# Macaron attention: the first q projection ahead of the scores on PE, and its rotation ahead of the maxima on DVE

## The chip, the cores and the metric

The kernel runs on one core of a Trainium2 chip. A core has five engines with a queue each: PE (TensorE, matmuls and transposes into PSUM), DVE (VectorE), ACT (ScalarE), POOL (GpSimd) and SP (SyncE, which here only issues DMAs). Each engine takes its instructions in program order; between engines there are semaphores. The metric is the device time of one execution in microseconds (us).

## What is computed

The input is 2 sequences of 1024 tokens with 128 features, in float32. Six sublayers follow each other, each behind a layer norm: a half-weighted "macaron" block, a linear attention, the same macaron block again, a mixture of experts, a full attention, and the experts again. The change touches the macaron block, which runs twice. It has 6 layers, each an attention over windows of 32 tokens in 16 heads and a gated feed-forward network. Its attention, cut to what matters:

```python
def attn_layer(x, Wqkv, qs, ksc, Wo):
    q, k, v = jnp.split(x @ Wqkv, 3, -1)             # 128 -> 3 x 1024
    q = l2norm(q) * qs                               # per head of 64
    k = l2norm(k) * ksc
    q = q * cos * scale + rotate_half(q) * sin * scale
    k = k * cos * inv + rotate_half(k) * sin * inv
    out = local_attention(q, k, v)                   # softmax over 64 keys
    return out @ Wo
...
for i in range(DEPTH):                               # 6
    x = attn_layer(shift_tokens(x), ...) + x
    x = ffn_layer(shift_tokens(x), ...) + x
```

## The kernel before

Tokens are cut into 16 tiles of 128. The macaron block is one pipeline over 6 x 16 = 96 tiles (`NT`), written out as 106 steps. Each engine runs the same loop `step(s)` in its own function, `macaron_pe`, `macaron_act`, `macaron_dve` and `macaron_pool`, and the order of the work is the order in which these functions issue it. In step s several tiles are in hand at once: tile u = s+2 is projected, squared and rotated, k = s+1 is scaled and transposed, t = s has its scores and softmax, o = s-1 is multiplied with the values and projected out, v = s-3 and z = s-4 have their layer norm for the feed-forward network.

A tile's q and k are each projected in two halves of 512 columns (the first and the second 32 of each head's 64 features), so `project_qk(u, q)` is called with q = 0 to 3, where 0 and 1 are the halves of q. Each of the four goes to a PSUM bank, ACT squares it out of there into `sq` (L554, for the norms), and DVE's `rotate(u, q)` (L666) multiplies it out of there with two rows of the rotary tables into `turn1` and `turn2`. POOL adds the two (L811) and, one step later, `scale(k, w)` (L795) multiplies the sum with the reciprocal norms `rn` into `qkr`, which PE transposes (L392). `turn1` and `turn2` exist once for q and once for k. That is why `rotate` has, for q = 0 and 2, a wait on the semaphore `qk_rotated` of the tile before:

```python
dve.wait_ge(sem("squared"), part(n, "squared", q))
if on(n - 1) and a == 0:
    dve.wait_ge(sem("qk_rotated"), part(n - 1, "qk_rotated", w))
```

POOL's order in a step is `scale(k, 0)`, `scale(k, 1)`, the normalisation of the probabilities (L823), the two adds (L811), a small `off` (L831) and the tables of the tile after (`ropes`, L805). The `off` waits for the end of DVE's Newton iteration in this step (L687), so that the next step's `scale(k, 0)` stands behind this iteration, the `off` and the `ropes`.

The scores of tile t (L417, 128 small matmuls) lie in two PSUM banks. DVE takes their row maxima (`nmax`, L724) and subtracts them into `scratch` (L729); ACT takes the exponential (L591); DVE sums it (`den`, L746) and inverts it (L749).

The feed-forward network works on groups of four tiles. Its gate matmuls (L462) with their gelus on ACT (L576, with a load of ACT's function table before and after, L579 behind it), its up matmuls (L469) with DVE's products (L702), and its output matmuls (L479) with DVE's addition (L708) stand at the end of three successive steps, and the fourth step has none. Below, a step is named by what the step before it ended with: behind a gate, behind an up, behind an out, and behind none.

`refill(b, ...)` is PE's bookkeeping of a PSUM bank: it waits until the last content was read. Bank 2 serves projections 0 and 3 and the first parts of gate and up.

Of the kernel before, what the change touches and what calls it, by code (L numbers as in the profile page):

```python
# [99 lines left out]
def build(nc, x_in, W, const, maskc, out):  # L100
    with ExitStack() as ctx:
# [233 lines left out]
        def on(n):  # L335
            return 0 <= n < NT
# [18 lines left out]
        def macaron_pe(pe, c):  # L355
# [9 lines left out]
            def project_qk(n, q):  # L365
                b = QK_BANK[q]
                refill(b, ("turned", part(n, "turned", q)))
                w, a = q // 2, q % 2
                w0 = INNER * w + RH * a
                pe.matmul(bank[b][:, :], xT[:, n // TPB % 2, bass.ts(n % TPB, P)],  # L370
                          wqkv[n // TILES % 2][:, INNER * w:INNER * w + INNER].rearrange(
                              "p (h a d) -> p h a d", a=2, d=RH)[:, :, a, :],
                          start=True, stop=True).then_inc(sem("projected"), 1)
# [110 lines left out]
            def step(s):  # L484
                x, u, k, t, o, v, z = s + 3, s + 2, s + 1, s, s - 1, s - 2, s - 4
                if s >= NT:
                    feed_forward(s)
                if on(t):
                    scores(t)
                if on(u):  # L490
                    if u % TILES == 0:
                        layer = DEPTH * c + u // TILES
                        pe.wait_ge(sem("attn_weights%d" % (layer % 2)), 16 * AW * (layer // 2 + 1))
                    pe.wait_ge(sem("xT_kept"), part(u, "xT_kept"))
                    for q in range(3):
                        project_qk(u, q)
                if on(o):
                    pe.wait_ge(sem("pT_kept"), part(o, "pT_kept", 1))
                    pe.wait_ge(sem("v_kept"), part(o, "v_kept", 1))
                    pe.wait_ge(sem("values_paired"), at.paired(o))  # L500
                    for i in range(2):
                        refill(OUT_BANK[i], ("aT_kept", part(o, "aT_kept", i)))
                    attend(o, 0)
                if on(k):
                    turn_qk(k, 0)
                if on(o):
                    attend(o, 1)
                if on(u):
                    project_qk(u, 3)
                if on(k):  # L510
                    project_v(k, 0)
                    turn_qk(k, 1)
                    turn_qk(k, 2)
                    project_v(k, 1)
                    turn_qk(k, 3)
                if on(t):
                    turn_p(t, 0)
                    turn_p(t, 1)
                if on(o):
                    project_out(o)  # L520
                if on(x) or on(z):
                    b = MIX_BANK
                    filled = []
                    if on(x):
                        filled.append(("xT_kept", part(x, "xT_kept")))
                    if on(z):
                        filled.append(("xnT_kept", part(z, "xnT_kept")))
                    refill(b, *filled)
                    if on(x):
                        if x >= TILES:  # L530
                            pe.wait_ge(sem("unit_added"), at.group((x - TILES) // 4, "unit_added"))
                        mm = pe.transpose(bank[b][:, 0:P], Y[:, x % TILES, :], ident[:, :])
                    if on(z):
                        pe.wait_ge(sem("unit_normed"), part(z, "unit_normed"))
                        mm = pe.transpose(bank[b][:, ZN_AT:ZN_AT + P], zn[:, :], ident[:, :])
                    mm.then_inc(sem("mixed"), 1)
                if s < NT:
                    feed_forward(s)
# [110 lines left out]
        def macaron_dve(dve, c):  # L649
# [67 lines left out]
            def step(s):  # L717
                u, t, o, v, z = s + 2, s, s - 1, s - 3, s - 4
                if s >= NT:
                    feed_forward(s)  # L720
                if on(t):
                    dve.wait_ge(sem("scores"), part(t, "scores"))
                    both = psum[:, S_BANK[0]:S_BANK[0] + 2, :].rearrange("p a b -> p (a b)")
                    dve.tensor_reduce(nmax[:, :], both.rearrange("p (h k) -> p h k", k=NWIN), AX.X, ALU.max,  # L724
                                      negate=True).then_inc(sem("maxima"), 1)
                    dve.wait_ge(sem("maxima"), part(t, "maxima"))
                    if on(t - 1):
                        dve.wait_ge(sem("p_turned"), part(t - 1, "p_turned", 1))
                    dve.tensor_tensor(prob[:, :].rearrange("p (h e k) -> p e h k", e=2, k=NWIN),  # L729
                                      both.rearrange("p (e h k) -> p e h k", e=2, k=NWIN),  # L730
                                      nmax[:, :].rearrange("p (e h) -> p e h", e=2).unsqueeze(3).broadcast_to(
                                          [P, 2, PAIRS, NWIN]), ALU.add).then_inc(sem("centred"), 1)
                if on(v):
                    dve.wait_ge(sem("shifted%d" % (v % 2)), at.shifted(v))
                    dve.bn_stats(st6[:, 0, :], Y[:, v % TILES, 0:HALF])
                    dve.bn_stats(st6[:, 1, :], zs[:, v % 2, :]).then_inc(sem("unit_stats"), 1)
                if on(u):
                    rotate(u, 0)
                if on(v):
                    dve.wait_ge(sem("unit_stats"), part(v, "unit_stats"))  # L740
                    if on(z):
                        dve.wait_ge(sem("unit_offset"), part(z, "unit_offset"))
                    dve.bn_aggr(mv[:, :], st6[:, :, :]).then_inc(sem("unit_moments"), 1)
                if on(t):
                    dve.wait_ge(sem("exp_done"), part(t, "exp_done"))
                    dve.tensor_reduce(den[:, :], prob[:, :].rearrange("p (h k) -> p h k", k=NWIN), AX.X,  # L746
                                      ALU.add).then_inc(sem("totals"), 1)
                    dve.wait_ge(sem("totals"), part(t, "totals"))
                    dve.reciprocal(rden[:, :], den[:, :]).then_inc(sem("inverted"), 1)  # L749
                if on(u):  # L750
                    rotate(u, 1)
                    rotate(u, 2)
                    rotate(u, 3)
                if s > FIRST_STEP:
                    dve.wait_ge(sem("rnorm"), at.step(s - 1))
                if on(v):
                    dve.wait_ge(sem("unit_moments"), part(v, "unit_moments"))
                    dve.tensor_scalar(ss[:, 32:33], mv[:, 1:2], LN_EPS, 64.0 / 9.0, ALU.add, ALU.mult).then_inc(
                        sem("unit_var"), 1)
                if on(u):  # L760
                    lengths(u, 0)
                    lengths(u, 1)
                    dve.wait_ge(sem("summed"), part(u, "summed", 1))
                    dve.tensor_scalar(ss[:, 0:32], ss[:, 0:32], 1e-24, None, ALU.max).then_inc(sem("norms_squared"), 1)
                    dve.wait_ge(sem("norms_squared"), part(u, "norms_squared"))
                if on(v):
                    dve.wait_ge(sem("unit_var"), part(v, "unit_var"))
                if on(z):
                    dve.wait_ge(sem("unit_normed"), part(z, "unit_normed"))
                if on(u - 1):  # L770
                    dve.wait_ge(sem("qk_rotated"), part(u - 1, "qk_rotated", 1))
                dve.tensor_scalar(rn[:, :].bitcast(I32), ss[:, :].bitcast(I32), -0.5, MAGIC, ALU.mult,
                                  ALU.add).then_inc(sem("guessed"), 1)
                dve.wait_ge(sem("guessed"), at.step(s))
                rsqrt(s)
                if on(o):
                    dve.wait_ge(sem("attn_out"), part(o, "attn_out"))
                    dve.tensor_tensor(Y[:, o % TILES, :], bank[WO_BANK][:, 0:D], Y[:, o % TILES, :],
                                      ALU.add).then_inc(sem("attn_added"), 1)
                if s < NT:  # L780
                    feed_forward(s)
# [871 lines left out]
```

## Time and profile before

| | |
|---|---|
| median of 3 runs | 4118.94 us (4118.94 to 4139.54) |
| the profiled execution | 4144.42 us |
| its span, first to last instruction | 4142.6 us |
| PE busy | 3870.5 us (93%) |
| DVE busy | 3321.1 us (80%) |
| ACT busy | 2742.4 us (66%) |
| POOL busy | 2224.1 us (54%) |
| mean granted TensorE clock | 0.953 of full speed |

The busy times are sums over the whole span, so they don't say which engine another waits for. The chain of work that ended last is followed back from the last instruction; the profile puts 63% of it on PE and 27% on DVE. In rows of the timeline, "x6" means six instructions merged into one row, the first number is the start in us from the span's start, the second the length in us, and the bracket at the end says how long the engine sat idle before the row and what ended that.

### The profile page before, as it was taken

How to read it: one execution, taken by the hardware profiler on the slowest of the kernel's cores; microseconds unless marked ns; L12 is line 12 of the kernel's file. 1: busy time of each engine (PE TensorE's matmuls, PEld its weight loads, DVE VectorE, ACT ScalarE, POOL GpSimd, SP SyncE). 2: the span in 40 equal slices, each digit the busy share in tenths (PEclk: the TensorE clock that was granted, in tenths of full speed). 3: DMA queues.
4: the chain of work that ended last, by engine and by line, in shares of the span. 5: the costliest groups of instructions: out<-in, count | busy, mean ns of one | idle time of the engine just before them, and what ended most of it. 6: DMA issues, size and time to landing. Idle time of an engine off the chain costs nothing.

```text
span 4142.6 us, 151779 instructions
## 1 busy us (share of the span) xinstructions
PE 3870.5 (93%) x65521; PEld 2410.0 (58%) x65521; DVE 3321.1 (80%) x6608; ACT 2742.4 (66%) x4984; POOL 2224.1 (54%) x1394
## 2 busy tenths in 40 slices
PE   6999999999999999589999999999999977999985
PEld 3666666666666666356666666666666654333333
DVE  7988888888888888588888888888888865577745
ACT  4777777777767676167777777777777742466662
POOL 4766666666666665077666666666666630000000
PEclk8999999999999999799999999999999987599996
DMA  3112121121121211012211211212111110000000
GB/s 103 41 35 57 40 57 40 40 57 40 35 57 40 57 38 43 23 29 45 51 41 40 57 40 40 57 40 57 35 43 38 35 26 0 1 1 1 1 1 11
DMA packets 138056, 154.51 MB, mean 37 GB/s; under 512 B 74392, under 2 KB 97320, under 8 KB 135728
## 3 DMA queue, kind: packets, MB, share of 16 engines
q1 hardware_dynamic: 137392, 144.81, 15.2%
q8 instruction: 520, 8.52, 0.9%
q14 instruction: 144, 1.18, 0.1%
HBM read 36.71 MB, written 1.05 MB: 9 GB/s over the span
## 4 chain that ended last, share of the span: by engine, by line
PE 63%; DVE 27%; issue 6%; ACT 2%; POOL 0%; DVEq 0%; SPq 0%; POOLq 0%; DMA 0%; ACTq 0%
DVE turn L666 10%; PE psum L381 10%; PE psum L449 8%; PE psum L392 8%; PE psum L417 7%; DVE nmax L724 5%; DVE den L746 5%; PE psum L441 4%; PE psum L1297 3%; PE psum L462 3%; PE psum L1285 3%; PE psum L469 3%; PE psum L479 3%; PE psum L370 2%; PE psum L1287 2%
## 5 line engine op out<-in xcount | busy, mean ns | idle before, releaser
L666 DVE TENSOR_TENSOR turn<-psum,ropes 128x512 f32<-128x512 f32 x1536 | 938.5, 672 | 31.4 <-ACT sq L554 27.1
L811 POOL TENSOR_TENSOR turn<-turn 128x1024 f32<-128x1024 f32 x384 | 904.6, 2377 | 32.6 <-DVE turn L666 32.5
L554 ACT ACTIVATE sq<-psum 128x512 f32<-128x512 f32 x768 | 451.5, 594 | 500.3 <-PE psum L370 498.9
L370 PE MATMUL psum<-wqkv,xT 128*128 128x512 f32 x1536 | 773.2, 626 | 8.5 <-DVE turn L666 6.8
L795 POOL TENSOR_TENSOR qkr<-turn,rn 128x1024 f32<-128x1024 f32 x384 | 727.9, 1918 | 17.3 <-DVE rn L687 17.2
L823 POOL TENSOR_TENSOR scratch<-scratch,rden 128x1024 f32<-128x1024 f32 x192 | 365.7, 1904 | 657.4 <-DVE rden L749 657.4
L392 PEld LDWEIGHTS psum<-ident,qkr 128*128 128x128 f32 x3072 | 329.4, 142 | 334.5 <-ACT kT L563 156.3
L392 PE MATMUL psum<-ident,qkr 128*128 128x128 f32 x3072 | 467.0, 285 | 6.7 <-POOL qkr L795 6.0
L692 DVE TENSOR_REDUCE ss<-sq 128x16 f32<-128x1024 f32 x384 | 447.9, 1207 | 0.0
L428 PEld LDWEIGHTS psum<-scratch,Vs 64*64 64x64 f32 x12288 | 330.4, 135 | 197.6 <-issue 197.2
L381 PE MATMUL psum<-wqkv,xT 128*64 128x512 f32 x1536 | 420.2, 626 | 23.2 <-DVE turn L666 6.1
L1423 DVE TENSOR_REDUCE gel<-psum 128x1 f32<-128x1024 f32 x256 | 303.9, 1220 | 150.8 <-PE psum L1266 149.4
L724 DVE TENSOR_REDUCE nmax<-psum 128x16 f32<-128x1024 f32 x192 | 235.0, 1224 | 232.2 <-PE psum L417 231.9
L428 PE MATMUL psum<-scratch,Vs 64*64 64x32 f32 x12288 | 395.6, 223 | 21.5 <-issue 21.5
L370 PEld LDWEIGHTS psum<-wqkv,xT 128*128 128x128 f32 x1536 | 263.7, 191 | 224.2 <-issue 182.2
L428 PE MATMUL psum<-scratch,V 64*64 64x32 f32 x12288 | 388.2, 220 | 0.5 <-issue 0.5
L449 PE MATMUL psum<-wo,aT 128*128 128x128 f32 x3072 | 377.5, 276 | 2.6 <-ACT aT L607 2.6
L449 PEld LDWEIGHTS psum<-wo,aT 128*128 128x128 f32 x3072 | 361.2, 193 | 2.8 <-ACT aT L607 2.8
L567 ACT ACTIVATE V<-psum 128x512 f32<-128x512 f32 x384 | 229.7, 598 | 190.8 <-PE psum L381 190.8
L428 PEld LDWEIGHTS psum<-scratch,V 64*64 64x64 f32 x12288 | 332.8, 137 | 0.6 <-issue 0.6
L417 PEld LDWEIGHTS psum<-kT,qT 64*32 64x32 f32 x24576 | 255.4, 105 | 91.1 <-issue 72.1
L417 PE MATMUL psum<-kT,qT 64*32 64x64 f32 (+1 forms) x24576 | 287.0, 225 | 4.5 <-ACT psum L625 3.5
(193 smaller groups left out, 6536.4 us busy)
## 6 DMA issues: line engine op xcount, KB each, us to landing
Vs<-V SPq DMA_DIRECT2D x384, 128.0 KB
Vs<-V SPq DMA_DIRECT2D x768, 64.0 KB
wqkv<-in_L_ffn_Wqkv_dram SPq DMA_DIRECT2D x12, 1536.0 KB
wo<-in_L_ffn_Wo_dram SPq DMA_DIRECT2D x48, 128.0 KB
zs<-Y SPq DMA_DIRECT2D x192, 31.8 KB
w<-in_L_ffn_W_dram SPq DMA_DIRECT2D x12, 341.0 KB
zs<-Y SPq DMA_DIRECT2D x168, 0.2 KB
w<-in_L_ffn_W_dram SPq DMA_DIRECT2D x12, 128.0 KB
```

The costliest lines, as they stand in the source:

```text
L370: pe.matmul(bank[b][:, :], xT[:, n // TPB % 2, bass.ts(n % TPB, P)], wqkv[n // TILES % 2][:, INNER * w:INNER * w + INNER].rearrange("p (h ...
L381: mm = pe.matmul(bank[b][DH * e:DH * e + DH, :], xT[:, n // TPB % 2, t0:t0 + 64], wv[:, :, e, :], start=True, stop=True, skip_group_check= ...
L392: mm = pe.transpose(bank[b][:, P * j:P * j + P], qkr[:, w, P * p:P * p + P], ident[:, :])
L417: mm = pe.matmul(out, q, keys, start=False, stop=True, skip_group_check=True)
L428: mm = pe.matmul(bank[OUT_BANK[e]][o0:o0 + DH, P * i + WIN * w:P * i + WIN * w + WIN], v[r0:r0 + NWIN, w // 2, p, :], pT[r0:r0 + NWIN, p, ...
L449: mm = pe.matmul(bank[WO_BANK][:, 0:D], aT[:, p, :], wo[n // TILES % 2][:, p, :], start=(p == 0), stop=(p == PAIRS - 1))
L554: act.activation(sq[:, q // 2, q % 2, :, :], bank[QK_BANK[q]][:, :].rearrange("p (h d) -> p h d", d=RH), ACT.Square).then_inc(sem("squared ...
L666: e = dve.tensor_tensor(dst, src, tab.unsqueeze(1).broadcast_to([P, HEADS, RH]), ALU.mult)
L692: dve.tensor_reduce(ss[:, 16 * w:16 * w + 16], sq[:, w, :, :, :].rearrange("p a h d -> p h a d"), AX.XY, ALU.add).then_inc(sem("summed"), 1)
L724: dve.tensor_reduce(nmax[:, :], both.rearrange("p (h k) -> p h k", k=NWIN), AX.X, ALU.max, negate=True).then_inc(sem("maxima"), 1)
L795: pool.tensor_tensor(qkr[:, w, :].rearrange("p (h a d) -> p a h d", a=2, d=RH), turn1[:, w, :, :, :], r.unsqueeze(1).unsqueeze(3).broadcas ...
L811: pool.tensor_tensor(t1, t1, turn2[:, w, :, :, :].rearrange("p a h d -> p (a h d)"), ALU.add).then_inc(sem("added"), 1)
```

## The change

PE issues `project_qk(u, 0)` ahead of `scores(t)`, and projections 1 and 2 stay behind them. DVE issues `rotate(u, 0)` as the first thing of the step (behind a feed-forward part only in the last steps), ahead of the maxima. ACT's and POOL's programs and all waits inside the moved functions stay as they are.

```diff
@@ macaron_pe, step(s)
-                if on(t):
-                    scores(t)
                 if on(u):
                     if u % TILES == 0:
                         layer = DEPTH * c + u // TILES
                         pe.wait_ge(sem("attn_weights%d" % (layer % 2)), 16 * AW * (layer // 2 + 1))
                     pe.wait_ge(sem("xT_kept"), part(u, "xT_kept"))
-                    for q in range(3):
-                        project_qk(u, q)
+                    project_qk(u, 0)
+                if on(t):
+                    scores(t)
+                if on(u):
+                    project_qk(u, 1)
+                    project_qk(u, 2)
@@ macaron_dve, step(s)
+                if on(u):
+                    rotate(u, 0)
                 if on(t):
                     dve.wait_ge(sem("scores"), part(t, "scores"))
...
-                if on(u):
-                    rotate(u, 0)
                 if on(v):
                     dve.wait_ge(sem("unit_stats"), part(v, "unit_stats"))
```

On PE, at the border of two steps behind an out (the transposes L532 and L535 and the output matmuls L479 close the old step; `kT,qT` are the scores, `wqkv1,xT` the projections), this stood there before:

```order
L535 MATMUL psum<-ident,zn 128x128 [waits unit_normed]
L479 MATMUL psum<-w20,gT 128x128 [waits gated,qk_kept]
L479 MATMUL psum<-w20,gT 128x128 x3
L417 MATMUL psum<-kT,qT 32x64 [waits qk_kept,masked]
L417 MATMUL psum<-kT,qT 32x64 x63
L370 MATMUL psum<-wqkv1,xT 128x512 [waits turned,xT_kept]
L370 MATMUL psum<-wqkv1,xT 128x512 [waits v_kept] x2
```

And this stands there now:

```order
L537 MATMUL psum<-ident,zn 128x128 [waits unit_normed]
L479 MATMUL psum<-w20,gT 128x128 [waits gated,qk_kept]
L479 MATMUL psum<-w20,gT 128x128 x3
L370 MATMUL psum<-wqkv1,xT 128x512 [waits turned,xT_kept]
L417 MATMUL psum<-kT,qT 32x64 [waits qk_kept,masked]
L417 MATMUL psum<-kT,qT 32x64 x63
L370 MATMUL psum<-wqkv1,xT 128x512 [waits v_kept] x2
```

One projection of 512 columns has moved ahead of the scores.

On DVE, from the end of the Newton iteration (L687; L689 now) and the up products (L702; L704 now) into a step behind an up, this stood there before:

```order
L687 SCALAR_TENSOR_TENSOR rn<-rt,rn 128x33 [waits newton]
L778 TENSOR_TENSOR Y<-psum,Y 128x128 [waits attn_out]
L702 SCALAR_TENSOR_TENSOR gT<-psum,b1,gel 128x512 [waits gelu,unit_up] x2
L702 SCALAR_TENSOR_TENSOR gT<-psum,b1,gel 85x512 [waits gelu,unit_up]
L724 TENSOR_REDUCE nmax<-psum 128x16 [waits scores]
L729 TENSOR_TENSOR scratch<-psum,nmax 128x2x8x64 [waits p_turned,maxima]
L735 BN_STATS st6<-Y 128x6 [waits shifted1]
L736 BN_STATS st6<-zs 128x6
L666 TENSOR_TENSOR turn1<-psum,ropes0 128x512 [waits ropes_scaled,qk_rotated,squared]
L666 TENSOR_TENSOR turn2<-psum,ropes0 128x512
L743 BN_AGGR mv<-st6 128x2 [waits unit_offset,unit_stats]
L746 TENSOR_REDUCE den<-scratch 128x16 [waits exp_done]
```

And this stands there now:

```order
L689 SCALAR_TENSOR_TENSOR rn<-rt,rn 128x33 [waits newton]
L780 TENSOR_TENSOR Y<-psum,Y 128x128 [waits attn_out]
L704 SCALAR_TENSOR_TENSOR gT<-psum,b1,gel 128x512 [waits gelu,unit_up] x2
L704 SCALAR_TENSOR_TENSOR gT<-psum,b1,gel 85x512 [waits gelu,unit_up]
L668 TENSOR_TENSOR turn1<-psum,ropes0 128x512 [waits ropes_scaled,qk_rotated,squared]
L668 TENSOR_TENSOR turn2<-psum,ropes0 128x512
L728 TENSOR_REDUCE nmax<-psum 128x16 [waits scores]
L733 TENSOR_TENSOR scratch<-psum,nmax 128x2x8x64 [waits p_turned,maxima]
L739 BN_STATS st6<-Y 128x6 [waits shifted1]
L740 BN_STATS st6<-zs 128x6
L745 BN_AGGR mv<-st6 128x2 [waits unit_offset,unit_stats]
L748 TENSOR_REDUCE den<-scratch 128x16 [waits exp_done]
```

The two rotations, with their three waits, have moved ahead of the maxima, and nothing is left between the centring (L729; L733 now) and the sum of the exponentials but the small statistics.

## Rows read from the trace of the kernel before

**Rows 1.** Who waited for whom (us in total, times, longest us), and the page's part 5
```profile
L724 DVE TENSOR_REDUCE nmax<-psum 128x16 f32<-128x1024 f32 x192 | 235.0, 1224 | 232.2 <-PE psum L417 231.9
PEld psum L381 <- DVE turn L666: 176.6, 190, 3.6
```
**Rows 2.** The chain that ended last, in order of time, one step
```profile
1039.93 1.23 DVE turn L666 x2
1041.21 1.08 PE psum L381 x4
...
1051.97 1.19 DVE turn L666 x2
```
**Rows 3.** Timeline of DVE, the step behind none, and the other three kinds' maxima
```profile
1017.17 1.22 DVE L724 TENSOR_REDUCE nmax<-psum 128x16 f32<-128x1024 f32 x1 [0.67 <-PE psum L417]
...
1034.60 1.23 DVE L724 TENSOR_REDUCE nmax<-psum 128x16 f32<-128x1024 f32 x1 [0.83 <-PE psum L417]
...
1049.23 1.22 DVE L724 TENSOR_REDUCE nmax<-psum 128x16 f32<-128x1024 f32 x1 [0.49 <-PE psum L417]
1050.49 1.22 DVE L729 TENSOR_TENSOR scratch<-psum,nmax 128x1024 f32<-128x1024 f32 x1
...
1053.20 1.16 DVE L746 TENSOR_REDUCE den<-scratch 128x16 f32<-128x1024 f32 x1
...
1054.57 3.61 DVE L666 TENSOR_TENSOR turn<-psum,ropes 128x512 f32<-128x512 f32 x6
...
1066.44 1.23 DVE L724 TENSOR_REDUCE nmax<-psum 128x16 f32<-128x1024 f32 x1 [3.09 <-PE psum L417]
```
**Rows 4.** Timeline of PE: scores behind up, out and none; the step behind none
```profile
1015.65 1.48 PE L417 MATMUL psum<-kT,qT 64*32 64x64 f32 x128
...
1032.97 1.59 PE L417 MATMUL psum<-kT,qT 64*32 64x64 f32 x128
...
1047.72 1.48 PE L417 MATMUL psum<-kT,qT 64*32 64x64 f32 x128
1049.13 2.84 PE L370 MATMUL psum<-wqkv,xT 128*128 128x512 f32 x6
...
1054.62 1.12 PE L370 MATMUL psum<-wqkv,xT 128*128 128x512 f32 x2
1055.84 1.08 PE L381 MATMUL psum<-wqkv,xT 128*64 128x512 f32 x4
...
1059.38 1.04 PE L441 MATMUL psum<-ident,scratch 128*128 128x128 f32 x8
```
**Rows 5.** Timeline of ACT: the step behind none, and the squares behind a gate
```profile
1050.29 0.60 ACT L554 ACTIVATE sq<-psum 128x512 f32<-128x512 f32 x1 [1.42 <-PE psum L370]
...
1051.75 1.06 ACT L591 ACTIVATE scratch<-scratch 128x1024 f32<-128x1024 f32 x1
...
1068.19 1.09 ACT L554 ACTIVATE sq<-psum 128x512 f32<-128x512 f32 x2
```
**Rows 6.** Timeline of POOL: the border into the step behind none
```profile
1048.64 0.27 POOL L831 TENSOR_SCALAR off<-mv,rn 128x1 f32<-128x1 f32 x1 [1.96 <-DVE rn L687]
...
1049.54 3.79 POOL L795 TENSOR_TENSOR qkr<-turn,rn 128x1024 f32<-128x1024 f32 x2
```
**Rows 7.** Timeline where the second macaron block begins: DVE waits for the exponential
```profile
1788.62 1.06 ACT L591 ACTIVATE scratch<-scratch 128x1024 f32<-128x1024 f32 x1
1789.71 1.22 DVE L746 TENSOR_REDUCE den<-scratch 128x16 f32<-128x1024 f32 x1 [1.23 <-ACT scratch L591]
```
**Rows 8.** Timeline of PE behind two waits at the beginnings of the blocks
```profile
66.28 1.97 PE L381 MATMUL psum<-wqkv,xT 128*64 128x512 f32 x4 [1.45 <-DVE turn L666]
...
1792.41 1.27 PE L381 MATMUL psum<-wqkv,xT 128*64 128x512 f32 x4 [2.75 <-DVE turn L666]
...
1797.52 1.04 PE L441 MATMUL psum<-ident,scratch 128*128 128x128 f32 x8
```
**Rows 9.** PE's busy time, granted clock and DMA in stretches of 1 us
```profile
1794.00:1795.00 1.00, 1.00 (x7) 0.50 0.00 0
```

## The prediction

> **What bounds the kernel now.** The page's busy shares don't settle it, so I read the waits first. The largest visible wait of DVE in the macaron block is the one for the scores, 231.9 us before 192 maxima, 1.2 us a step; and PE in turn waits 176.6 us, about 0.9 us a step, for DVE's rotation before it projects the values [rows 1]. Two engines that wait for each other in every step are one loop. The chain of waits shows it: DVE's rotation 1, then PE's value projection at once, from there PE's tail of the step up to the next scores, the maxima, and over rotation 0 to the next rotation 1 [rows 2]. The step before is therefore (rotation 1 to scores, on PE) + (scores) + (maxima to rotation 1, on DVE), and anything put on this loop costs its full length. The DVE wait for scores that the change fills with a rotation is real, but it is a link of the loop, not free time beside it.
>
> **The change, part by part.** No instruction is added or removed. I take one group of four steps from the middle of the first block, in which each kind of step occurs once.
>
> *What is saved.* Today rotation 0 lies between the centring and the sum of the exponentials, from the maxima to rotation 1 it is 1054.57 - 1049.23 = 5.34 us [rows 3]. Without rotation 0 the sum must wait for ACT: maxima to centring 1.26 [rows 3], centring to the start of the exponential 1051.75 - 1050.49 = 1.26 [rows 3, 5], exponential to sum 1.09, as where DVE really waited for it [rows 7], sum to rotation 1 1.37 [rows 3]. That is 4.98 us. So of the 1.19 us of rotation 0 [rows 2] only 0.36 us come off this stretch; the rest was cover for the exponential, and the cover is gone.
>
> *What is added ahead of the maxima.* Rotation 0 now needs three things before it may start, and the maxima stand behind it in DVE's queue even when the scores are ready.
> (a) Its projection and square. From a projection's start to the start of its square it is 1050.29 - 1049.13 = 1.16 us, the square takes 0.60 [rows 4, 5], I add 0.03 to hand it on (the exponential needed that [rows 7]) and 1.19 for the rotation: 2.98 us from PE's start to the maxima. Now it is the scores alone, about 1.5 us. On PE itself the scores end two passes (0.86 us) later, at about 2.4, which this hides.
> (b) The buffer. `turn1` and `turn2` of q are read by POOL's `scale(k, 0)`. Behind none POOL comes to it at 1049.54, with `off` and `ropes` ahead of it, and two take 3.79, so the first ends at 1051.44 [rows 6]. Today nobody sees that, because rotation 0 comes 2.7 us behind the start of the maxima. Now it stands between DVE and maxima that could have started at 1049.23.
> (c) Behind a gate, ACT. The gelus and two table loads lie ahead of the first square in ACT's queue, and it starts only at 1068.19 [rows 5], 1.75 us behind the start of the maxima today.
>
> New starts of the maxima, against those of today [rows 3 to 6]:
> - behind none: 1051.44 + 0.06 + 1.19 = 1052.69 for 1049.23, +3.46, net of the 0.36 +3.10
> - behind a gate: 1068.19 + 0.60 + 0.03 + 1.19 = 1070.01 for 1066.44, +3.57, net +3.21
> - behind an up: 1015.65 + 2.98 = 1018.63 for 1017.17, +1.46, net +1.10
> - behind an out: 1032.97 + 2.98 = 1035.95 for 1034.60, +1.35, net +0.99
>
> Everything from rotation 1 on (PE's tail, DVE's reductions and Newton iteration, POOL's adds, ACT's copies and gelus) hangs on rotation 1 as before, so a delay is not made up later in the step; the periods just grow. In the up step the products L702 free bank 2 before PE gets to it, which I cost at nothing; the cover is PE's own matmuls, without it it is some tenths.
>
> In a block rotation 0 and maxima share steps s = 0 to 93: 30 behind none, 22 behind a gate, 21 behind an up, 21 behind an out. For two blocks: 60 x 3.10 + 44 x 3.21 + 42 x 1.10 + 42 x 0.99 = 186 + 141 + 46 + 42 = **415 us**. SP's queue is not moved, and its pairing DMAs get more time, which can give back a few us.
>
> *The clock.* PE's wait before the value projections grows with the same amounts. Behind none, projection 3 starts at 1054.62, its two passes take 0.86, and the next matmul starts at 1055.84 [rows 4]: 0.4 us of gap today, 3.5 then, 3.6 behind a gate, about 1.4 in the other two. What such waits do is shown where the blocks begin: behind a wait of 2.75 us the clock stood at 0.50, the lower of its two levels (1.2 GHz), while PE worked, and the way from the value projection to the transposes of the probabilities took 1797.52 - 1792.41 = 5.11 us, against 1059.38 - 1055.84 = 3.54 in the middle: 1.57 us lost [rows 4, 8, 9]. Behind a wait of 1.45 us the same projection took 1.97 instead of 1.08 [rows 8], so even that can be enough. The bounds for the block's middle: 0 (today's gaps of 0.4 us leave the clock at full) and all of them. A fall costs where PE's tail or ACT behind it decides the next maxima, in tails with gate, up or out: 44 + 44 + 42 steps. In the tail without one, PE has 1052.69 - (1047.72 + 2.98) = 1.99 us in hand behind POOL, and 1.57 fits in. Those with gate or up (88) follow a long gap, those with out a short one. I take nine in ten of the 88 and a quarter of the 42, at 1.5 us because a fall sometimes begins before the wait ends: 90 x 1.5 = **135 us**. The most is 130 x 1.57 = 204 us.
>
> The Trainium skill, "TensorE: Matmul & The Clock Gate", section "HAM oscillation", tells of a kernel in which PE had to wait in every turn of a loop and came back at half rate in every one. By that rule all 88 long gaps fall and the term is 88 x 1.57 = 138 us; a reading of the middle of the blocks alone, where gaps are 0.4 us, would leave it at 0. The rows at the blocks' beginnings side with the page.
>
> **Sum.** 415 + 135 = 550 us. On the profiled execution's own 4144.4 us that is 4694; the median lies 25.5 us lower, so I forecast **4669 us**.
>
> **The rivals.**
> 1. *The loop as above, the clock stays at 2.4 GHz* (PE's attention matmuls in front of the gap may count for enough): 4119 + 415 = 4534 us. For it: both rows of a fall come from the first steps of a block, where these attention matmuls are missing. Against it: one of these waits was only 1.45 us [rows 8]. Chance 0.20.
> 2. *More than forecast*: every gap brings a fall, or one outlasts the tail and slows the next scores too. From 4119 + 415 + 204 = 4738 us up, to some 4850 if half of the falls cost double. Chance 0.12.
> 3. *POOL and ACT don't stand in the way*, because their work moves ahead when steps get longer; then only (a) is left in all kinds: 188 x 1.1 = 207, 4326 us. Against it: POOL's `scale` is tied to this loop's Newton iteration through `off`, which waited 1.96 us for it [rows 6]. Chance 0.07.
> 4. *The other side, faster*: the rotation fits into DVE's wait for the scores and the maxima don't get later, so 0.36 us a step are won, 188 x 0.36 = 68 us: 4051 us. It decides if both the square and `qk_rotated` are there 1.2 us before the scores end. Behind a gate DVE did sit idle for 3.09 us [rows 3], but there the square would have to end at 1065.2 and ends at 1068.8, and behind none the buffer would have to be free at 1048.0 and is at 1051.4. Chance 0.03.
> 5. *No effect*, the two amounts cancelling or the loop not being the bound: 4119 us. The chain of waits speaks against it. Chance 0.02.
>
> My own case has 0.56, with 4600 to 4738 as its range. A measurement of this kernel tells about 0.5% from no change. Cases 1, 2, 3 and mine are all slower: slower 0.95, same 0.02, faster 0.03. The range for 8 in 10 takes in mine and most of 1 and of 2: from 4520 to 4770 us.
>
> **What the changed profile would show.** The wait of the maxima for the scores is gone from the list (231.9 us), since the maxima now follow the rotation directly. In its place rotation 0 waits for `qkr` (POOL L795) behind none, some 2.7 us each time, and for the square elsewhere, most behind a gate. The sum of the exponentials waits some 0.7 us for ACT in every step. PE's wait for the rotation before the value projections grows from 0.9 us to about 3 on average. In the middle of a block four steps take 3.10 + 3.21 + 1.10 + 0.99 = 8.4 us more than now, or 11.5 with the clock's part (two long gaps at nine in ten and a short one at a quarter, 1.5 us each), and the granted clock there is below 1.00. The forecast is wrong if rotation 0 doesn't wait for POOL, or if four steps grow by less than 8 us; if they grow by just 8.4, rival 1 holds.

## The result, and the profile after

The changed kernel takes 4574.11 us (median of 4, 4553.43 to 4584.89), the kernel before, run beside it, 4129.24 us (4118.94 to 4140.34). The ratio is 1.108 with a 95% interval of [1.104, 1.112], slower by 445 us. The forecast was 4669 us with a range of 4520 to 4770: the direction and the range held, the size was 95 us too high, and rival 1 (the same loop without the clock's part, 4534 us) came closer.

The waits of the changed kernel, in us in total, times, longest:

```profile
PEld psum L381 <- DVE turn L668: 468.8, 194, 5.2
DVE turn L668 <- ACT sq L556: 347.5, 144, 6.3
PE psum L381 <- DVE turn L668: 311.5, 180, 4.3
DVE turn L668 <- POOL qkr L797: 150.2, 56, 2.8
DVE den L748 <- ACT scratch L593: 122.1, 192, 1.1
```

The wait of the maxima for the scores, 231.9 us in [rows 1], has shrunk to 2.4 us. In its place DVE waits 498 us ahead of rotations: 144 times for the square, 56 times for POOL's scaling of the tile before, and about nine in ten of these waits stand ahead of rotation 0. A third one, 0.62 us in most steps, is the bubble in front of the sum of the exponentials. PE's wait for DVE before the value projections has grown from 176.6 to 468.8 us, which is 2.4 us each and not the 3 us forecast.

One group of steps in the timeline of DVE: behind none, behind a gate, behind an up, behind an out.

```profile
1098.40 1.22 DVE L728 TENSOR_REDUCE nmax<-psum 128x16 f32<-128x1024 f32 x1
...
1115.02 1.29 DVE L668 TENSOR_TENSOR turn<-psum,ropes 128x512 f32<-128x512 f32 x2 [2.81 <-POOL qkr L797]
1116.22 1.22 DVE L728 TENSOR_REDUCE nmax<-psum 128x16 f32<-128x1024 f32 x1
...
1119.82 1.22 DVE L748 TENSOR_REDUCE den<-scratch 128x16 f32<-128x1024 f32 x1 [0.62 <-ACT scratch L593]
...
1121.24 3.62 DVE L668 TENSOR_TENSOR turn<-psum,ropes 128x512 f32<-128x512 f32 x6
...
1137.07 1.29 DVE L668 TENSOR_TENSOR turn<-psum,ropes 128x512 f32<-128x512 f32 x2 [6.29 <-ACT sq L556]
1138.28 1.22 DVE L728 TENSOR_REDUCE nmax<-psum 128x16 f32<-128x1024 f32 x1
...
1155.26 1.29 DVE L668 TENSOR_TENSOR turn<-psum,ropes 128x512 f32<-128x512 f32 x2 [0.74 <-ACT sq L556]
1156.46 1.22 DVE L728 TENSOR_REDUCE nmax<-psum 128x16 f32<-128x1024 f32 x1
...
1173.54 1.29 DVE L668 TENSOR_TENSOR turn<-psum,ropes 128x512 f32<-128x512 f32 x2 [0.80 <-ACT sq L556]
1174.75 1.22 DVE L728 TENSOR_REDUCE nmax<-psum 128x16 f32<-128x1024 f32 x1
```

Every maxima row now starts the moment its rotation is through; what the rotation waited for stands in the bracket. From the starts of all 192 maxima I took the period of each step, that is from the start before to its own, and sorted them by kind (the first maxima of a block have no period, so it is 58 of the 60 behind none):

| step behind | before, median | worked out | after, median | steps |
|---|---|---|---|---|
| none | 14.63 | 17.73 | 17.83 | 60 |
| a gate | 17.22 | 20.43 | 20.48 | 44 |
| an up | 17.22 | 18.32 | 18.18 | 42 |
| an out | 17.32 | 18.31 | 18.29 | 42 |

The medians account for 60 x 3.20 + 44 x 3.26 + 42 x 0.96 + 42 x 0.97 = 416 us. The rest are steps above their kind's median. Behind a gate 16 of 44 lie at 22.0 to 23.4 us, behind an up 9 at 19.5 to 21.1. PE's timeline shows the one behind a gate of the group above, with PE's granted clock in 1 us:

```profile
1111.92 1.12 PE L370 MATMUL psum<-wqkv,xT 128*128 128x512 f32 x2 [0.65 <-ACT xT L635]
...
1119.05 1.13 PE L370 MATMUL psum<-wqkv,xT 128*128 128x512 f32 x2
1122.52 1.75 PE L381 MATMUL psum<-wqkv,xT 128*64 128x512 f32 x4 [2.34 <-DVE turn L668]
1124.20 1.97 PE L392 MATMUL psum<-ident,qkr 128*128 128x128 f32 x8
...
1127.64 1.04 PE L441 MATMUL psum<-ident,scratch 128*128 128x128 f32 x8
```
```profile
1124.00:1125.00 1.00, 1.00 (x6) 0.50 0.87 194
```

Behind the wait the clock is at the lower level, and from the value projection to the transposes of the probabilities it takes 1127.64 - 1122.52 = 5.12 us, as at the block's beginning [rows 8], instead of 3.54 [rows 4]. Only it happened much less often than I had taken it to. In the record of the granted clock there are 33 falls (154 us) between the first and the last maxima of the two blocks, against 6 (37 us) in the kernel before. Each of the 16 long periods behind a gate and of the 9 behind an up has such a fall in it, and no other period of these two kinds lies more than 0.7 us above its median.

### The profile page after: what moved, and what is told of

Its sections match the earlier page's. It is cut to its first block, busy times and chain, and to the rows that moved or that the text cites. A ratio compares the mean times of both kernels' runs of the same rounds, so it can differ in the third digit from the quotient of the medians.

```text
span 4568.1 us, 151779 instructions
## 1 busy us (share of the span) xinstructions
PE 3933.8 (86%) x65521; PEld 2414.2 (53%) x65521; DVE 3369.3 (74%) x6608; ACT 2731.0 (60%) x4984; POOL 2221.4 (49%) x1394
## 4 chain that ended last, share of the span: by engine, by line
PE 43%; DVE 25%; ACT 13%; POOL 10%; issue 8%; DVEq 0%; SPq 0%; POOLq 0%; DMA 0%; ACTq 0%
PE psum L381 7%; DVE turn L668 7%; PE psum L449 6%; PE psum L392 6%; DVE scratch L733 5%; DVE den L748 5%; DVE nmax L728 5%; POOL turn L813 4%; ACT scratch L593 4%; PE psum L370 3%; PE psum L1299 3%; PE psum L469 3%; PE psum L441 3%; PE psum L1287 3%; PE psum L479 3%
## 5 line engine op out<-in xcount | busy, mean ns | idle before, releaser
L370 PE MATMUL psum<-wqkv,xT 128*128 128x512 f32 x1536 | 810.1, 630 | 78.0 <-ACT xT L635 44.2
L381 PE MATMUL psum<-wqkv,xT 128*64 128x512 f32 x1536 | 450.3, 667 | 311.5 <-DVE turn L668 311.5
L392 PEld LDWEIGHTS psum<-ident,qkr 128*128 128x128 f32 x3072 | 349.6, 148 | 363.2 <-issue 193.5
L392 PE MATMUL psum<-ident,qkr 128*128 128x128 f32 x3072 | 490.4, 296 | 8.5 <-POOL qkr L797 7.7
L593 ACT ACTIVATE scratch<-scratch 128x1024 f32<-128x1024 f32 x192 | 203.0, 1057 | 387.6 <-DVE scratch L733 387.6
L370 PEld LDWEIGHTS psum<-wqkv,xT 128*128 128x128 f32 x1536 | 251.2, 190 | 275.7 <-issue 191.9
L381 PEld LDWEIGHTS psum<-wqkv,xT 128*64 128x64 f32 x1536 | 79.6, 141 | 506.9 <-DVE turn L668 468.8
```

The source lines that it names most:

```text
L381: mm = pe.matmul(bank[b][DH * e:DH * e + DH, :], xT[:, n // TPB % 2, t0:t0 + 64], wv[:, :, e, :], start=True, stop=True, skip_group_check= ...
L392: mm = pe.transpose(bank[b][:, P * j:P * j + P], qkr[:, w, P * p:P * p + P], ident[:, :])
L593: act.activation(prob[:, :], prob[:, :], ACT.Exp).then_inc(sem("exp_done"), 1)
```

## The experiments

### The two halves of the change alone

PE's half (DVE as before):

```diff
-                if on(u):
-                    rotate(u, 0)          # ahead of the maxima
...
+                if on(u):
+                    rotate(u, 0)          # behind the statistics, as before
```

> Only PE's part of the change: projection 0 ahead of the scores, rotation 0 in its old place behind the centring. My theory (one loop over PE's tail, scores, maxima and rotation 1): the maxima start 0.86 us later in every kind of step, because two passes lie ahead of the scores, and the cover of the exponential stays; 188 x 0.86 = 162 us, and behind a gate projection 0 waits about 0.5 us more for the first gelu to empty bank 2 (44 x 0.5 = 22 us): ratio 1.044, about 4310 us. Rival, that PE's order costs nothing because DVE's or POOL's work sets the step: 1.00, 4129 us.

Measured: 4359.49 us, ratio 1.058 [1.053, 1.063]. Slower as expected, but by 237 us and not 181. The periods tell where: behind up and out 18.08 and 18.18, +0.86 as worked out; behind none 16.40 and behind a gate 18.96, +1.77 and +1.74. PE's timeline of this run has the cause:

```profile
1127.86 1.12 PE L370 MATMUL psum<-wqkv,xT 128*128 128x512 f32 x2 [0.65 <-ACT xT L635]
1128.92 1.48 PE L417 MATMUL psum<-kT,qT 64*32 64x64 f32 x128
...
1146.85 1.10 PE L370 MATMUL psum<-wqkv,xT 128*128 128x512 f32 x2 [0.64 <-ACT gel L578]
```

Behind none the moved projection needs the transposed input `xT`, which ACT copies at the very end of the step before. As long as the scores came first, they hid that copy. My reasons missed this wait altogether. Behind a gate the 0.64 us is the wait for the first gelu, which I had expected here at 0.5, but which the prediction had left out. Behind none it is more than the bracket says: in this run the transpose ahead of the moved projection starts at 1126.94 and the scores at 1128.92, 1.98 us later, against 0.21 us from transpose to scores before (1047.51 and 1047.72), so 1.77 us came in between, which is what the period grew by. In the full change both waits are there as well (the row at 1111.92 above), but the maxima wait longer for POOL and ACT.

DVE's half (PE as before): `rotate(u, 0)` ahead of the maxima, with projections 0 to 2 behind the scores.

> Only DVE's part: rotation 0 ahead of the maxima, projection 0 behind the scores as before. My theory: the square can only follow scores and projection, so from PE's start to the maxima it is 1.41 + 1.16 + 0.63 + 1.19 = 4.39 us behind an up or out, +2.5 us net each (84 steps, 210 us); behind none and a gate POOL and ACT set the time as in the full change, +3.2 and +3.26 (192 + 143 us); with some 60 us for the clock about 4735 us, ratio 1.147. Slower than the full change, so PE's part is a help inside it. Rival, that the two parts add up (full change 445 = PE's part 180 + DVE's 265): 4394 us, ratio 1.064.

Measured: 4884.4 us, ratio 1.185 [1.183, 1.187]. The two halves don't add up: DVE's alone costs 762 us, the full change 445, so inside the change PE's half is a remedy, since without it the square has to wait for scores and projection. The shortest steady periods, 19.79 behind an up and 19.89 behind an out, are the 17.22 and 17.32 + 2.5 of the theory, but more than half of these steps lie at 22.2 and 21.5, and the mean granted clock is 0.901 (0.953 before). PE sits idle 2.9 us on average in front of the value projections (541 us in 188 waits; in the full change 311.5 us in 180, 1.7 us), and the clock fell 141 times in the two blocks. The falls are what the expectation was short by: the periods without a fall have medians of 17.83 behind none and 20.48 behind a gate, as expected, and 19.79 and 19.89 behind up and out; those with one are 0.8 to 2.3 us longer behind none and 1.4 to 2.9 us in the other kinds.

### The buffer

```diff
+        other1 = sb("other1", [P, 2, HEADS, RH])
...
-                if on(n - 1) and a == 0:
-                    dve.wait_ge(sem("qk_rotated"), part(n - 1, "qk_rotated", w))
+                if on(n - 1) and w and a == 0:
+                    dve.wait_ge(sem("qk_rotated"), part(n - 1, "qk_rotated", w))
+                if on(n - 1) and q == 0:
+                    dve.wait_ge(sem("added"), part(n - 1, "added", w))
+                    if on(n - 2):
+                        dve.wait_ge(sem("qk_rotated"), part(n - 2, "qk_rotated", w))
```

Odd tiles' `turn1` of q is `other1`, in rotation, add and scaling.

> The full change, with a second turn1 for q used by odd tiles, so that rotation 0 waits for the scaling of the tile two before instead of the one before. My theory: only the steps behind none change; there the maxima wait for the square instead of POOL, the period falls from 17.83 to 14.63 + 1.46 - 0.36 = 15.73 us, 60 x 2.1 = 126 us less than the full change: about 4448 us, ratio 1.077; the other kinds keep 20.48, 18.18, 18.29. Rival, that POOL's wait is a symptom and something else (PE's tail, the exponential) takes its place: 4574 us, ratio 1.108.

Measured: 4493.29 us, ratio 1.089 [1.088, 1.091], 78 us below the full change by the ratios. Behind none the period is 16.52 (from 17.83), so the buffer was what bound these steps. Most of the 0.8 us missing to 15.73 is the wait for `xT`, 0.65 us, which stands in PE's timeline of this run too. Behind a gate all periods are 20.48 now, the falls of the clock are gone there, and behind an up they have come: in 40 of 44 periods, with a median of 19.78 for 18.18, while the four without a fall keep 18.18. The first is no surprise, since PE's idle time in front of the value projections, in the steps whose tail holds the gates, went from 2.4 to 1.1 us. The second is: in the steps behind a gate it is 2.48 us in both runs, and brought 10 falls in 44 steps there and 40 here.

### The clock

Redundant copies of projection 3 into its own bank, ahead of it, keep PE at work in its gap:

```diff
+            def fill(n, times):
+                for _ in range(times):
+                    pe.matmul(bank[2][:, :], ...)        # projection 3, no increment
...
+                    if on(t):
+                        ...                              # the waits of bank 2
+                        fill(u, 3 if s < 9 or s % 4 < 2 else 1)
                     project_qk(u, 3)
```

> The full change, with redundant copies of projection 3 ahead of projection 3 on PE (three behind a gate and none, 2.6 us, one behind up and out, 0.86 us), into the same bank, so that PE's gap before the value projections is short; nothing else moves. My theory: the periods above the medians (gate 12 times 22.1 and 4 times 23.4 for 20.48, up 9 times 19.6 to 21.1 for 18.18) are falls of the clock to 1.2 GHz; they vanish and the medians stay: 45 us less than the full change, about 4530 us, ratio 1.097. Rival, that the long periods have another cause (late pairing DMAs, weight loads): they stay, 4574 us, ratio 1.108, or more if the copies get in the way.

Measured: 4553.19 us, ratio 1.108 [1.101, 1.115], by itself inconclusive. In the first block, from 100 us to its last maxima, the time at the lower clock fell from 72 us (14 falls) to 3 us (1 fall), and the long periods behind a gate went from 16 to 2; but 18 steps behind up and out now lie more than 0.8 us above their median. So I took away the copies in the short gaps, and left the three in the long ones:

> The full change with the three redundant copies of projection 3 only where the gap is long (behind a gate and behind none); behind up and out nothing is added. In the run with copies everywhere the falls of the clock were gone, but some steps behind up and out had grown by about 1.3 us. My theory: those came from the copy in the short gap; now both kinds keep 18.18 and 18.29, the gate's long periods are gone, and the time is that of the full change less its falls: 4574 - 45 = about 4530 us, ratio 1.097. Rival, that the clock's falls cost nothing that the copies don't cost too: 4555 to 4574 us, ratio 1.103 to 1.108.

Measured: 4541.57 us, ratio 1.100 [1.098, 1.1025], against 1.108 [1.104, 1.112]. The time at the lower clock in the same stretch is 17 us (3 falls), and the medians are 17.84, 20.60, 18.23 and 18.29, close to those of the full change. So taking away the falls won about 33 us (by the two intervals, give or take 18), and with the copies' own 0.12 us behind a gate (44 times, 5 us) that is some 38 us. The full change's own periods say a little more: behind a gate the 16 with a fall lie 30.8 us in total above their median, behind an up the 10 with a fall 18.9 us, together 50 us, where I had put 135.

Long steps behind up and out (6 each) stayed without any copies there, so my reading of them was wrong. Those behind an up have no fall in them. Four of the six follow a step behind a gate in which PE stood still inside its scores, where the profile names no releaser:

```profile
759.15 0.31 PE L423 MATMUL psum<-kT,qT 64*32 64x64 f32 x7 [1.31 <-issue]
```

The full change has three such stops behind a gate, and no long step behind them: PE's idle time in front of the value projections is 0.88, 1.11 and 1.26 us in these three for 2.48 in the others, so it took them up. The copies fill just this idle time. That a stop then goes through to the next maxima, and that the copies pay back a part of the 50 us in this way, is my reading of the rows; no run tests it.

### ACT behind a gate

The load of the exponential's table moves from behind the gelus to behind squares 0 and 1:

```diff
@@ feed_forward(s), ACT
-                    if s < NT:
-                        act.activation(warm[:, g % 2:g % 2 + 1], ones[:, :], ACT.Exp)...
@@ step(s), ACT
                     square(u, 0)
                     square(u, 1)
+                g = gate_group(s - 1)
+                if g is not None and s - 1 < NT:
+                    act.activation(warm[:, g % 2:g % 2 + 1], ones[:, :], ACT.Exp)...
```

> The full change, with ACT's load of the exponential's table moved from behind the gelus to behind squares 0 and 1 of the next step. My theory: behind a gate the maxima hang on the first square, which hangs on ACT; it starts up to 1.5 us earlier, the period falls from 20.48 to about 19.0 us, 44 x 1.5 = 66 us less than the full change, with fewer falls of the clock as the gap shrinks: about 4505 us, ratio 1.092. The load then lies where ACT waits 2.7 us for the centring. Rival, that behind a gate PE (which waits for the first gelu to empty bank 2) sets the time: no change against 4574 us, ratio 1.108.

Measured: 4539.76 us, ratio 1.102 [1.097, 1.107]. By the ratios that is 24 us below the full change, with intervals that overlap, so the periods have to tell. The mechanism shows: the 15 periods behind a gate without a fall of the clock have a median of 19.06, the 19.0 of the theory. In the other 29 the clock fell, in the full change in 16, and they lie mostly around 20.6. Behind an up the median rose by 0.28 us to 18.46. Half of the 66 us expected, or somewhat more, went back in these two ways. I had expected fewer falls as PE's gap behind a gate shrinks; there they are indeed gone (none for 10), but they came in the steps before.

### Rotation 1 into the bubble

In the full change DVE waits 0.62 us for the exponential. Here rotation 1 fills that:

```diff
+                if on(u):
+                    rotate(u, 1)              # ahead of the sum of the exponentials
...
                 if on(u):
-                    rotate(u, 1)
                     rotate(u, 2)
```

> The full change, and rotation 1 ahead of the sum of the exponentials, where the full change leaves DVE waiting 0.6 us for ACT. My theory: from the maxima to rotation 1 it is then 2.8 us instead of 5.0 and the loop over PE's tail is no longer the longest; the one over POOL is: maxima to the end of the Newton iteration 13.93 - 1.19 = 12.74, to the free buffer 2.89, hand-over and rotation 0 1.25, together 16.9 us behind none, up and out; behind a gate ACT's chain gives 15.44 + 2.8 = 18.2 us. Against before +2.25 x 60, +1.0 x 44, -0.34 x 42, -0.44 x 42 = +147 us: about 4275 us, ratio 1.036. Rival, that only PE's loop counts and each step wins 2.2 us: 4574 - 188 x 2.2 = 4160 us, ratio 1.008.

Measured: 4507.94 us, ratio 1.093 [1.089, 1.097]; neither theory. The periods were 18.12 behind none, up and out, and 18.96 behind a gate. And the same edit on the kernel before:

> The kernel before with one edit only: rotation 1 directly behind rotation 0, ahead of the sum of the exponentials. It shortens the same loop from the other end: from the maxima to rotation 1 3.9 us instead of 5.3. My theory: PE stops waiting for DVE before the value projections, and its own work becomes the bound, of which 0.4 us a step were gap: 188 x 0.4 = 75 us faster, 4050 us, ratio 0.982. The normalised probabilities come 1.2 us later to PE, which has about 2.3 us in hand there. Rival, that DVE or POOL binds as closely as PE: ratio 1.00; a second rival, that the later probabilities bind: ratio 1.01.

Measured: 4137.99 us, ratio 1.001 [0.999, 1.003]. Behind a gate it won 0.6 us (16.63), behind none it lost 0.6 (15.22). The expected gain had gone somewhere, and one row of DVE's timeline is long that was not touched. From POOL's timeline and DVE's, in this run:

```profile
1017.47 4.68 POOL L811 TENSOR_TENSOR turn<-turn 128x1024 f32<-128x1024 f32 x2
```
```profile
1020.21 1.98 DVE L764 TENSOR_SCALAR ss<-ss 128x32 f32<-128x32 f32 x1
1022.23 0.18 DVE L772 TENSOR_SCALAR rn<-ss 128x33 int32<-128x33 int32 x1
```

A clamp of 32 elements takes 1.98 us, and ends at 1022.19, as POOL's second add does (1022.15). In the kernel before it is the same with a shorter overlap:

```profile
1007.32 4.72 POOL L811 TENSOR_TENSOR turn<-turn 128x1024 f32<-128x1024 f32 x2
```
```profile
1011.25 0.82 DVE L764 TENSOR_SCALAR ss<-ss 128x32 f32<-128x32 f32 x1
```

1012.04 and 1012.07. The third theory: the Newton iteration hangs on POOL, whose normalisation and two adds start with the inverted sums; moving rotation 1 ahead delays exactly those. If so, one add ahead of the normalisation helps, since rotation 1 is there early now:

```diff
@@ step(s), POOL
+                if on(u):
+                    add(u, 0)
                 if on(t):
                     pool.wait_ge(sem("inverted"), part(t, "inverted"))
...
                 if on(u):
-                    add(u, 0)
                     add(u, 1)
```

> The kernel before with rotation 1 directly behind rotation 0 (as in the run that stayed at 1.001), and POOL's first add ahead of its normalisation of the probabilities instead of behind it. In that run DVE's small clamp of the norms (L764, 128x32) took 1.98 us in the median where it takes 0.81 before and 0.18 at its shortest, and it always ended when POOL's second add ended; so my theory is that the end of the Newton iteration hangs on POOL's three operations behind the inverted sums, and that this is what took the gain. With one add ahead, POOL is through before DVE comes to L764: it takes 0.2 us again, the iteration ends about 13.2 us behind the maxima (13.9 before, 14.7 in that run), and PE's own work is the bound, 0.4 us a step below before: ratio 0.98, about 4050 us. Rival, that L764 is long for a reason of its own: it keeps its 2 us and the ratio stays at 1.00.

Measured: 4088.29 us, ratio 0.991 [0.988, 0.994]: faster than both kernels, by half of what I expected. The clamp by minimum/median/maximum ns, in the kernel before, with rotation 1 alone, and with POOL's order:

```profile
L764 DVE TENSOR_SCALAR ss<-ss x192: 180/814/867, 43.6 to 3340.4; 128x32 f32<-128x32 f32 x192
```
```profile
L764 DVE TENSOR_SCALAR ss<-ss x192: 180/1983/2064, 43.3 to 3347.6; 128x32 f32<-128x32 f32 x192
```
```profile
L764 DVE TENSOR_SCALAR ss<-ss x192: 180/503/643, 43.7 to 3301.0; 128x32 f32<-128x32 f32 x192
```

It follows POOL's order, not its own work. It isn't at 0.18 because POOL's last add still reaches into it. The periods are 14.46, 17.04, 17.04 and 17.15, 0.17 to 0.18 us below before each, and PE's wait for DVE before the value projections is down to 13.5 us in total, from 176.6, while DVE waits 245.0 us for the scores. One waits and the other doesn't, so PE's own work is the bound here. With rotation 1 alone neither waited much (84.4 and 81.3 us).

> The full change with rotation 1 ahead of the sum of the exponentials and POOL's first add ahead of its normalisation. Rotation 1 alone gave periods of 18.12 behind none, up and out and 18.96 behind a gate, where I had expected 16.9 for the former. My theory: L767 (the clamp) waits for POOL's second add; without that wait the end of the Newton iteration comes about 1.5 us earlier in the loop over POOL, and the three kinds fall to about 17.3 or below, the gate, which hangs on ACT, keeps 18.96: 0.8 to 1.2 us for 144 steps, 4508 - 145 = about 4365 us, ratio 1.058. Rival, that POOL's time is the same however it is ordered: 1.093.

Measured: 4339.86 us, ratio 1.051 [1.046, 1.057]. Behind none, up and out the medians are 16.65, 16.98 and 17.43 (18.12 without POOL's edit), behind a gate 18.99. The part of the full change that is left is the one through ACT and the buffer, as the theory has it.

## Why the prediction was right, and what in it was wrong

**The loop** was right. The four periods worked out lie within 0.14 us of the measured medians, and their sum, 415 us, is what the medians give, 416. Both halves of the exchange showed up as they were put: rotation 0 taken out from between centring and sum saves little (maxima to rotation 1 is 1121.24 - 1116.22 = 5.02 us after, 4.98 worked out, 5.34 before), because ACT's exponential comes to light; and rotation 0 ahead of the maxima waits for the square or for the buffer.

**What releases rotation 0** was right: POOL behind none (shown by the second buffer), ACT behind a gate (by the later table load, where the clock stays up), projection and square elsewhere (by the run with DVE's half, which adds the scores to that way and costs the 2.5 us expected).

**The clock** was the mis-sized term: "nine in ten of the 88 and a quarter of the 42" falls at 1.5 us were to cost 135 us. Behind the gaps that counted (the 88) there were 26 falls and not 79, and they cost 50 us by the periods, some 38 by the run that filled the long gaps. The cost of one fall was right (5.12 us for 3.54, and 1.4 to 1.6 us in a period; the falls that lasted 6.8 us instead of 3.4 cost 2.8 to 2.9), how often it happens was not. Two rows from the first steps of a block, where no attention matmuls stand ahead of the wait, don't carry over to the steps with them, as rival 1 had it. The measured 4574 us lies below the 4600 at which the forecast's own case began; the range held because it took in rival 1's 4534 us as well. The prediction's own sign for that rival, four steps that grow by 8.4 us, is what the medians show (the means, falls included, give 9.0).

**The gap itself** was mis-sized too. Reckoned as the prediction did it, it is 1122.52 - (1119.05 + 0.86) = 2.6 us behind none and 2.75 behind a gate, for the 3.5 and 3.6 forecast, and 1.3 in the other two, as forecast. The missing 0.9 us is where PE now waits ahead of projection 0, for `xT` or for the first gelu. So the section "HAM oscillation" of the Trainium skill's "TensorE: Matmul & The Clock Gate" is no base for 88 falls: the kernel that it tells of waited some 3 to 5 us in each turn, and PE here sat idle for 2.4 to 2.5. Nor does the length of the wait settle it here: 2.4 us brought 16 falls in 44 steps, 2.5 us 10 in 44 or 40 in 44 (the second buffer), and with DVE's half 2.7 us brought 39 in 44 ahead of the gates and 3.4 us behind them only 25 in 44. What decides which waits bring a fall stays open.

**"Hangs on rotation 1 as before"** was right in its size and wrong in its reason. The Newton iteration isn't DVE's own work behind rotation 1; it waits in L764 for POOL's adds, which hang on the inverted sums. In the full change sums and rotation 1 move together, so the number came out; as soon as they moved apart, in the two runs with rotation 1, it failed.

**Not seen** was the wait for `xT` behind none, 0.65 us, and about 0.6 us for the first gelu behind a gate. Both lie beside longer waits of DVE in the full change, so they add nothing to the periods, but they shorten the gap in front of the value projections.

**What remains.** Between the first and the last maxima of each block the profiles give 3601.1 - 3160.6 = 440.5 us, of the 445 measured. For these 190 periods the medians make 414 us. The excess over the medians grew by 30 us behind a gate and 16 behind an up, the falls of the clock, and shrank by 5 behind none and by 15 behind an out. That adds up. The 15 us come from steps that are long in both kernels, one every sixteenth. In the kernel before:

```profile
884.16 0.32 PE L428 MATMUL psum<-scratch,Vs 64*64 64x32 f32 x8 [1.99 <-issue]
```

PE stops ahead of its first attention matmul, where the program waits for the pairing DMAs among others; the profile names no releaser, and no run tests it. In four of these steps before, and in two after, a fall of the clock follows, and each of these six periods lies 4.8 to 6.8 us above the median. These six steps alone make 21.2 us of the excess before and 12.7 after, a good half of the 15 us.

## What to carry over

An idle stretch in front of an engine's wait is no room for more work if that wait is a link of the loop that sets the step: ask what the moved instruction itself needs, at its new place, from every other engine, write down the time of each, and check what it covered at its old place. Two halves of a change may be a cost and a remedy rather than two costs; only runs of each alone tell. And if a tiny instruction is long, look at what ends at the same time on another engine.

## What the runs showed of the hardware

A DVE tensor_scalar of 128x32 from SBUF to SBUF takes 0.18 us alone and up to 2.06 us beside a POOL tensor_tensor of 128x1024; it ends with POOL's instruction, while DVE's multiplications out of PSUM (L666, 0.68 us each) run at their usual length beside it. The profile shows the clamp as busy and long, not as waiting. The Trainium skill says in "SBUF — State Buffer", section "SBUF: two separate sides", that DVE and GpSimd have a pair of ports in common, which a DVE instruction needs in a two-port mode or with two inputs in SBUF, and which one instruction holds to its end while the other waits. These rows agree; the runs here show the wait and how it moves with POOL's order, not the ports, nor whether the clamp runs in such a mode.

Which steps see TensorE's clock at 1.2 GHz depends on the steps around them, and not on the length of PE's wait alone: with the second buffer a wait of 2.48 us, the same as in the full change, went from 10 falls to 40 in 44 steps, and the median of the period behind an up from 18.18 to 19.78 us, with nothing changed in these steps.
